# Three products of constants ahead of each turn of queries and of keys in the last batch of attention

## The chip, the cores and the metric

The kernel runs on one NeuronCore of one Trainium2 chip. The metric is the device time of one execution in microseconds (us); for each kernel the median of several runs is given. TensorE multiplies matrices, VectorE, ScalarE and GpSimd work on elements, and SyncE issues most of the DMAs. The five engines run their own instruction streams and wait for each other by semaphores. The results of TensorE land in PSUM, which has eight banks of 512 32-bit columns.

## The reference

The program computes a stack of six blocks on x of shape 4 x 512 x 256 (four batches of 512 tokens): half a mixture of experts (8 experts, the best 2 of each token), a causal attention with 16 heads of 16 columns and rotary positions, the same mixture of experts again, a gated feed-forward block with a Walsh-Hadamard transform, a linear attention on random features, and the feed-forward block again. Each block reads the layer-normalised x and adds to x. The change lies in the causal attention, which is, cut to what matters:

```
q, k, v = split((layernorm(x) @ Wqkv + bqkv).reshape(b, s, 3, H, hd))
q, k = rot(q), rot(k)
scores = einsum('bthd,bshd->bhts', q, k * scale) + causal_mask
ctx = einsum('bhts,bshd->bthd', softmax(scores), v).reshape(b, s, d)
x = x + ctx @ Wout + bout
```

Nothing that the change adds is read by any of this.

## The kernel before, in words

The stages run one after the other, each as a block of five instruction streams written out by hand. The attention stage is `attention_stage` (from L1129). It goes through the four batches, and in each batch through eight pairs of heads; a pair of heads is numbered w, 0 to 31 (`PAIR` is 8, `LAST` is 3, so the last batch is w = 24 to 31). A pair takes three steps t of one software pipeline (`STEPS` is 3): 24 steps a batch, 96 in all, and then a tail.

On TensorE the order is a fixed list (the loop `for t in range(ALL + LAG + 5)` in `_(pe)`). In each step it issues `scores(t)` (queries times keys, for the row maxima, L1440), `shifted(t - 7)` (the transposed scores, which ScalarE then takes the exponentials of, L1455), in two of six steps `weigh` (probabilities times values, L1470), then in the first step of a pair `turn_q(s + 1)` and in the second `turn_k(s + 1)`. A turn is four transposes of 128x128 blocks into PSUM bank 4 (L1411), which ScalarE (`out_q`, L1722) or VectorE (`out_k`, L1872) copies to where `scores` and `shifted` read it. The turns of pair w stand in the steps of pair w - 1, and `scores` of pair w waits for both copies. The turn of keys waits for ScalarE's copy of the queries, since both turns use bank 4. VectorE masks the scores in PSUM and takes their row maxima (`maxima`, L1882) into the stack of queries; `scores(t)` waits for the maxima of step t - 1 in the same bank, and `turn_q(w)` for all maxima of pair w - 2. Two more turns of queries, w = 32 and 33, follow the last pair: they carry only the maxima, as the shifts of the softmax.

Between these, TensorE does the work of other batches. In the first three batches the steps hold the projections of the next batch: `turn_x` (L1374), `project_qk` (28 products of 512 columns, L1386 and L1389) and `project_v` (24 of 256 columns, L1396). From the second batch on they hold the end of the batch before: `turn_sums` (L1480), `turn_context` (L1494), `project_half` (L1504). The last batch has no next batch to project. It has, instead, the first pieces of the experts stage that follows: `turn_after` of batches 0 and 1 (eight transposes each, L199) and `choice.logits_of` of the same (the router's logits, products of 8 columns, L235).

SyncE's queue holds, in order, for each w a wait for the copy of the queries of w + 2 and two small DMAs that place the shift (`place_shift`, L1257), and in the last batch between them the loads of the next stage's first weights (`early`, L1272).

`spin(nc, g, bank, count)` (L369) issues `count` products of a constant (`g.ident`) with a constant (`g.column`), 128x128 32-bit floats each, into the first 128 columns of a PSUM bank. Nothing reads the result. The kernel before calls it in several places where TensorE would stand idle. In the trace each such product is two MATMUL records of L372.

Of the kernel before, what the change touches and what calls it, by code (L numbers as in the profile page):

```python
# [48 lines left out]
def f32(ap):  # L49
    return ap.bitcast(F32)  # L50
# [318 lines left out]
def spin(nc, g, bank, count):  # L369

    for _ in range(count):
        nc.tensor.matmul(g.ps[:, bank, 0:P], g.ident[:, :], g.column[:, :], start=True, stop=True)  # L372
# [777 lines left out]
def attention_stage(nc, g, ins):  # L1150
# [3 lines left out]
    with ExitStack() as ctx:  # L1154
# [61 lines left out]
        PAIR = H // 2  # L1216
        CARRY = 2
        part = lambda j: sum((BT - a) * P for a in range(j))
        LAST = BATCH - 1
# [150 lines left out]
        def _(pe):  # L1370
# [36 lines left out]
            def turn_stack(w, stack, bank, done):  # L1407
                b, hp = w // PAIR, w % PAIR
                for i in range(BT):
                    flat = f32(stack[min(b, LAST) % 2][:, i, :, :]).rearrange("p h c -> p (h c)")  # L1410
                    last = nc.tensor.transpose(g.ps[:, bank, i * P:(i + 1) * P], flat[:, hp * P:(hp + 1) * P],  # L1411
                                               g.ident[:, :])
                last.then_inc(done, 1)

            def turn_q(w):
                pe.wait_ge(lo_done, 4 * min(w // PAIR + 1, BATCH))
                if w:
                    pe.wait_ge(k_out, min(w, BATCH * PAIR))
                if w >= CARRY:
                    pe.wait_ge(max_done, 2 * STEPS * (w - CARRY + 1))  # L1420
                if w > BATCH * PAIR:
                    pe.wait_ge(q_out, w)
                turn_stack(w, q_stack, 4, q_ps)

            def turn_k(w):
                pe.wait_ge(q_out, w + 1)
                turn_stack(w, k_stack, 4, k_ps)

            def scores(t):
# [110 lines left out]
            for i in (2, 3):  # L1540
                pe.wait_ge(lo_done, i)
                spin(nc, g, 0, 10)
            turn_q(0)
            turn_k(0)
            for t in range(ALL + LAG + 5):
                b, u = t // WIDTH, t % WIDTH
# [17 lines left out]
                if step == 0 and s + 1 < BATCH * PAIR + CARRY:  # L1564
                    turn_q(s + 1)
                elif step == 1 and s + 1 < BATCH * PAIR:
                    turn_k(s + 1)
# [1276 lines left out]
```

## Time and profile before

| what | value |
|---|---|
| median of 3 runs | 1104.36 us |
| lowest and highest run | 1098.37 and 1105.86 us |
| span of the profiled execution | 1103.5 us |
| mean granted clock of TensorE in it, of full speed | 0.935 |
| busy time of TensorE (share of the span) | 1021.3 us (93%) |
| of VectorE | 711.2 us (64%) |
| of ScalarE | 452.3 us (41%) |
| of GpSimd | 431.8 us (39%) |

The span runs from the first to the last instruction of one profiled execution; the page gives no other time of that execution. The busy time of TensorE counts each product from its start to its modelled end, so products that follow each other closely overlap, and the time that one more product takes is better read from the distance between starts. The granted clock is the share of full speed (2.4 GHz) at which TensorE was clocked; it is 1.00 or 0.50 at any moment, and a stretch with a value between them held both. Times in rows are from the start of the span.

### The profile page before, as it was taken

How to read it: one execution, taken by the hardware profiler on the slowest of the kernel's cores; microseconds unless marked ns; L12 is line 12 of the kernel's file. 1: busy time of each engine (PE TensorE's matmuls, PEld its weight loads, DVE VectorE, ACT ScalarE, POOL GpSimd, SP SyncE).
4: the chain of work that ended last, by engine and by line, in shares of the span. 5: the costliest groups of instructions: out<-in, count | busy, mean ns of one | idle time of the engine just before them, and what ended most of it. 6: DMA issues, size and time to landing. Idle time of an engine off the chain costs nothing. (4 is left out here: it accounts for less than half of the span.)

```text
span 1103.5 us, 18327 instructions
## 1 busy us (share of the span) xinstructions
PE 1021.3 (93%) x6383; PEld 845.2 (77%) x6383; DVE 711.2 (64%) x1740; ACT 452.3 (41%) x772; POOL 431.8 (39%) x473
## 2 busy tenths in 40 slices
PE   8889995799999999988999989999888998899997
PEld 7878885655566665577888878888778986888886
DVE  5854443988798876556554367765549977566654
ACT  4524332346675755535443312323344543223222
POOL 3246655326363621205566400000159987200000
PEclk7699997978999987888999999999988999999999
DMA  9224424200000023126542150000010300000000
GB/s 327 87 74 138 167 77 137 77 1 2 3 2 20 2 82 121 39 65 230 211 144 92 67 201 1 1 1 1 11 67 1 77 1 1 1 2 20 20 20 20
DMA packets 39179, 71.97 MB, mean 65 GB/s; under 512 B 10610, under 2 KB 28082, under 8 KB 38836
## 3 DMA queue, kind: packets, MB, share of 16 engines
q1 hardware_dynamic: 29492, 48.25, 13.3%
q0 software_dynamic: 7488, 20.46, 5.6%
q10 hardware_dynamic: 2112, 2.10, 0.6%
q8 instruction: 55, 0.90, 0.3%
q14 instruction: 32, 0.26, 0.1%
HBM read 46.78 MB, written 23.87 MB: 64 GB/s over the span
## 5 line engine op out<-in xcount | busy, mean ns | idle before, releaser
L2202 PE MATMUL ps<-xt,w 128*128 128x512 f32 x768 | 191.4, 399 | 4.1 <-PEq L437 2.7
L2202 PEld LDWEIGHTS ps<-xt,w 128*128 128x128 f32 x768 | 141.4, 190 | 34.4 <-DVE xt L210 4.5
L1882 DVE CUSTOM_DVE_ANT_0 ps<-ps,att_mask 128x128 f32<-128x128 f32 (+3 forms) x256 | 119.2, 517 | 28.2 <-PE ps L1440 27.8
L2296 DVE TENSOR_TENSOR had_gated<-ps,had_sig 128x512 f32<-128x512 f32 x64 | 44.3, 692 | 108.7 <-ACT had_sig L2255 108.7
L2255 ACT ACTIVATE had_sig<-ps 128x512 f32<-128x512 f32 x64 | 38.3, 599 | 185.2 <-PE ps L2202 185.2
L676 POOL DMA_INDIRECT moe_xs<-xn_rows,moe_index x78 | 85.3, 1093 | 71.1 <-DVE moe_index L1071 42.9
L1743 ACT ACTIVATE att_early_probs<-ps 128x384 f32<-128x384 f32 (+1 forms) x192 | 91.1, 528 | 51.8 <-PE ps L1455 51.2
L771 PE MATMUL ps<-moe_w,moe_narrow_xb 128*128 x390 | 110.8, 398 | 0.0
L155 POOL TENSOR_TENSOR var_eps<-bn,eps 128x4 f32<-128x4 f32 x22 | 4.7, 216 | 266.0 <-DVE bn L118 251.5
L682 POOL DMA_INDIRECT made_rows<-moe_units_made,moe_index x78 | 77.6, 995 | 71.2 <-ACT moe_units_made L919 59.6
L1331 POOL TENSOR_SCALAR_AFFINE_SELECT att_early_probs<-att_early_probs 128x256 f32<-128x256 f32 x128 | 54.6, 441 | 114.4 <-ACT att_early_probs L1743 114.1
L1090 DVE TENSOR_TENSOR moe_narrow_xb<-ps,moe_narrow_xb 128x512 fp32r<-128x512 f32 (+1 forms) x40 | 27.1, 678 | 110.8 <-ACT moe_narrow_xb L901 110.8
L2216 PE MATMUL ps<-w,had_yhi 128*128 128x256 f32 x512 | 94.4, 282 | 1.8 <-DVE had_ylo L2308 1.8
L2216 PEld LDWEIGHTS ps<-w,had_yhi 128*128 128x128 f32 x512 | 82.5, 188 | 7.9 <-DVE had_ylo L2308 2.6
L771 PEld LDWEIGHTS ps<-moe_w,moe_narrow_xb 128*128 128x128 f32 x390 | 73.8, 189 | 15.4
L901 ACT ACTIVATE moe_narrow_xb<-ps 128x512 fp32r<-128x512 f32 (+1 forms) x40 | 23.5, 587 | 131.6 <-PE ps L753 131.5
L1440 PE MATMUL ps<-att_kt,att_qt 48*128 48x128 f32 (+3 forms) x256 | 67.3, 439 | 9.6 <-DVE att_q_stack L1882 6.1
L2216 PE MATMUL ps<-w,had_ylo 128*128 128x256 f32 x256 | 71.7, 280 | 0.0
L372 PE MATMUL ps<-column,ident 128*128 128x128 f32 x364 | 55.4, 323 | 17.5 <-DMA back<-made_rows 11.4
L2440 POOL TENSOR_TENSOR fea_inv_norm<-fea_norm,neg_half 128x24 f32<-128x24 f32 x16 | 66.9, 4183 | 7.4 <-DVE fea_norm L2696 7.4
L372 PEld LDWEIGHTS ps<-column,ident 128*128 128x128 f32 x364 | 53.5, 236 | 18.5 <-DMA back<-made_rows 11.6
L1440 PEld LDWEIGHTS ps<-att_kt,att_qt 48*128 48x128 f32 x256 | 33.9, 204 | 41.6 <-issue 23.5
(290 smaller groups left out, 2326.1 us busy)
## 6 DMA issues: line engine op xcount, KB each, us to landing
moe_w<-in_moe SPq DMA_DIRECT2D x12, 768.0 KB, 8.0
back<-made_rows SPq DMA_DIRECT2D x14, 512.0 KB, 6.3
x<-x_turned SPq DMA_DIRECT2D x8, 512.0 KB, 6.9
low_weights<-moe_w SPq DMA_DIRECT2D x4, 768.0 KB, 3.6
w_early<-in_moe SPq DMA_DIRECT2D x4, 768.0 KB, 4.5
w_early<-low_weights SPq DMA_DIRECT2D x4, 768.0 KB, 11.4
x<-in_x SPq DMA_DIRECT2D x4, 512.0 KB, 5.6
xn_rows<-moe_wide_xn SPq DMA_DIRECT2D x4, 512.0 KB, 11.4
```

The source lines that it names most:

```text
L372: nc.tensor.matmul(g.ps[:, bank, 0:P], g.ident[:, :], g.column[:, :], start=True, stop=True)
L676: nc.gpsimd.indirect_dma_start(out=xs[:, j % AHEAD, i, :], out_offset=None, in_=g.xn_dram[:, :], in_offset=at(0, 2 * j + i)).then_inc(gath ...
L682: nc.gpsimd.indirect_dma_start(out=g.made_dram[:, :], out_offset=at(1, 2 * j + i), in_=made[:, j % 2, i, :], in_offset=None) \
L771: last = nc.tensor.matmul(h_bank(j, i), xb[a][:, j % 2, i, k, :], weight(c), start=False, stop=(k == KC - 1 and c == 1))
L1331: last = nc.gpsimd.affine_select(block, block, [[0, 2], [1, P]], ALU.is_ge, 0.0, base=0, channel_multiplier=-1)
L1440: last = nc.tensor.matmul(g.ps[:, a, col:col + n], qt[at, w % 4, i * P:n], kt[at, w % 4, 0:n], start=True, stop=True)
L1743: nc.scalar.activation(probs[:, w % 3, a, at:at + n], g.ps[:, 2 + a, 0:n], ACT.Exp, scale=HD ** -0.5).then_inc(exp_done, 1)
L1882: last = nc.vector.tensor_tensor_reduce(g.ps[:, a, col:col + n], g.ps[:, a, col:col + n], mask[:, SEQ - n:SEQ], -1.0, 3.0e38, ALU.add, ALU ...
L2202: last = nc.tensor.matmul(g.ps[:, bank(n, half), :], w[a][:, k, c * P:(c + 1) * P], xt[low][:, b % 2, k, :], start=(k == 0 and q == 0), st ...
L2216: last = nc.tensor.matmul(o, a[:, n % 4, at], g.w2[w][:, c, :], start=(c == 0 and q == 0 and i % 2 == 0), stop=(c == HC - 1 and q == 2), s ...
L2296: nc.vector.tensor_tensor(gated[:, n % 2, :], g.ps[:, bank(n, 0), :], sig[:, n % 2, :], ALU.mult) \
L2440: nc.gpsimd.tensor_tensor(inv_norm[:, t % 4, :], norm2[:, t % 4, :], g.neg_half[:, 0:QKH], ALU.pow) \
```

## The change

Ahead of the four transposes of a turn, and behind the waits of that turn, TensorE issues three products of constants into bank 4, for all turns with w over 24. These are the turns of queries for w = 25 to 33 and the turns of keys for w = 25 to 31. The turn of w = 24, which stands in the steps of the batch before, stays as it is.

```
@@ -1420,10 +1420,14 @@
                     pe.wait_ge(max_done, 2 * STEPS * (w - CARRY + 1))
                 if w > BATCH * PAIR:
                     pe.wait_ge(q_out, w)
+                if w > LAST * PAIR:
+                    spin(nc, g, 4, 3)
                 turn_stack(w, q_stack, 4, q_ps)
 
             def turn_k(w):
                 pe.wait_ge(q_out, w + 1)
+                if w > LAST * PAIR:
+                    spin(nc, g, 4, 3)
                 turn_stack(w, k_stack, 4, k_ps)
```

## Rows read from the trace of the kernel before

**Rows 1.** The page: span, and TensorE's granted clock in 40 slices, in tenths.
```profile
span 1103.5 us, 18327 instructions
PEclk7699997978999987888999999999988999999999
```

**Rows 2.** Busy time by stretch of the attention stage; the first row names the columns.
```profile
core 0: us, PE busy (x) PEld busy (x) DVE busy (x) ACT busy (x) POOL busy (x), PEclk, DMA share, GB/s
335.50:392.80 57.30, 56.16 (x431) 35.70 (x430) 48.88 (x170) 38.49 (x80) 30.07 (x51) 1.00 0.04 11
392.80:455.90 63.10, 60.15 (x415) 38.74 (x414) 44.91 (x185) 32.21 (x64) 13.88 (x34) 0.78 0.27 89
...
404.70:414.60 9.90, 9.17 (x36) 6.58 (x36) 7.87 (x37) 4.60 (x10) 2.00 (x5) 0.50 0.45 149
...
421.80:431.60 9.80, 9.19 (x48) 5.63 (x47) 8.41 (x39) 5.78 (x12) 2.15 (x6) 0.50 0.39 119
...
442.00:448.60 6.60, 6.60 (x39) 3.93 (x39) 3.74 (x10) 2.80 (x7) 1.17 (x3) 0.50 0.01 2
...
459.50:462.50 3.00, 3.00 (x24) 1.53 (x20) 2.04 (x6) 0.41 (x2) 1.27 (x2) 0.50 0.53 175
```

**Rows 3.** All waits of TensorE's products, 392.8 to 474: us, times, longest.
```profile
PE ps L1440 <- DVE att_q_stack L1882: 2.7, 7, 0.7
PE ps L1455 <- ACT att_early_probs L1743: 1.1, 3, 0.5
PE ps L1470 <- POOL att_early_probs L1331: 0.4, 1, 0.4
```

**Rows 4.** Timeline, TensorE at full clock: start us, us, engine, line, xcount.
```profile
361.74 1.44 PE L1389 MATMUL ps<-wqkv,att_xt 128*128 128x512 f32 x5
363.10 0.50 PE L1440 MATMUL ps<-att_kt,att_qt 48*128 48x128 f32 x4
...
386.60 0.66 PE L1411 MATMUL ps<-ident,att_q_stack 128*128 128x128 f32 x4
387.01 0.96 PE L1396 MATMUL ps<-wqkv,att_xt 128*128 128x256 f32 x6
387.90 0.45 PE L1440 MATMUL ps<-att_kt,att_qt 48*128 48x384 f32 x2
...
396.06 1.04 PE L199 MATMUL ps<-ident,att_turns_after_xn 128*128 128x128 f32 x8
397.03 0.50 PE L1440 MATMUL ps<-att_kt,att_qt 48*128 48x512 f32 x2
...
401.75 1.85 PE L235 MATMUL ps<-gate_w,att_qk 128*128 128x8 f32 x16
403.52 0.45 PE L1440 MATMUL ps<-att_kt,att_qt 48*128 48x384 f32 x2
```

**Rows 5.** Timeline, one turn of keys at half clock and the next instruction.
```profile
411.42 1.12 PE L1411 MATMUL ps<-ident,att_k_stack 128*128 128x128 f32 x4
412.33 1.91 PE L199 MATMUL ps<-ident,att_turns_after_xn 128*128 128x128 f32 x8
```

**Rows 6.** Timeline: ten products of constants at full clock.
```profile
209.58 2.50 PE L372 MATMUL ps<-column,ident 128*128 128x128 f32 x20
```

**Rows 7.** Busy time in a stretch that holds only products of constants.
```profile
504.80:507.90 3.10, 3.10 (x14) 3.10 (x15) 3.00 (x8) 2.32 (x3) 2.28 (x3) 0.50 1.02 424
```

**Rows 8.** Next stage's first weights: their loads and first reader (ns min/median/max, first, last start).
```profile
L845 ACT ACTIVATE moe_w<-w_early x4: 1467/1468/1474, 495.1 to 499.2; 128x1536 fp32r<-128x1536 f32 x4
...
L1272 SPq DMA_DIRECT2D w_early<-in_moe x4: 525/581/581, 403.8 to 428.9; - x4
```

More of the change, by code:

```diff
@@ L1422, in turn_q @@
                     pe.wait_ge(q_out, w)
+                if w > LAST * PAIR:
+                    spin(nc, g, 4, 3)
                 turn_stack(w, q_stack, 4, q_ps)
@@ L1426, in turn_k @@
                 pe.wait_ge(q_out, w + 1)
+                if w > LAST * PAIR:
+                    spin(nc, g, 4, 3)
                 turn_stack(w, k_stack, 4, k_ps)
```

## The prediction

> **What bounds the kernel now.** I read the page first, for the share of each engine and the granted clock by slices [rows 1]. The 15th to 17th slices (386 to 469 us), the last part of the attention stage, stand at 8, 7 and 8 tenths, where the four before them stand at 9. I then cut that part into stretches by the granted clock [rows 2]. The third batch, w = 16 to 23, took 57.3 us, at a clock of 1.00 throughout; TensorE was busy for 56.16 us of it and VectorE for 48.88. The last batch, w = 24 to 31, took 63.1 us, at a mean clock of 0.78. It holds three of the four stretches at half clock, 9.9, 9.8 and 6.6 us long; the fourth, 3.0 us, lies just behind it. TensorE was busy for 60.15 us of the 63.1. So in both batches TensorE bounds the stage by and large, and the last batch, which has less arithmetic on TensorE, is the longer one because of its clock. The list of waits says the same: from the start of the last batch to 474 us TensorE's products stood idle for 4.2 us behind named releasers, 2.7 of it for VectorE's maxima [rows 3].
>
> Inside the half-clock stretches the picture is mixed. In the first two VectorE was busy for 7.87 of 9.9 us and 8.41 of 9.8 us, so a faster TensorE would soon wait for it there; in the third it was busy for only 3.74 of 6.6 [rows 2].
>
> **What the change adds.** Nine turns of queries and seven of keys get three products each: 48 products. Ten of them at full clock are 20 records in 2.50 us [rows 6]; less about 0.27 for the end of the last record that is (2.50 - 0.27) / 19 = 0.117 us a record and 0.235 us a product. At half clock 14 records took 3.10 us [rows 7], 0.221 a record and 0.44 a product. A turn's three products cost 0.70 us at full clock and 1.33 at half; all 48 cost 11.3 us at full clock.
>
> They stand on TensorE's queue behind the waits of the turn and ahead of its transposes. Behind them wait the copy of the turned block (ScalarE for queries, VectorE for keys), and then `scores` of the next steps. Time spent here is therefore on the path unless TensorE would have waited just after. It did wait for 4.2 us in all [rows 3], and that is the most that the products can hide in as the trace stands. At full clock there would be more room in the first two slow stretches: 9.9 - 7.87 = 2.0 and 9.8 - 8.41 = 1.4 us are what VectorE leaves, and TensorE's 9.17 and 9.19 us would shrink to some 5 each, so that up to 4 us of products in each would lie beside VectorE's work.
>
> No DMA is issued by the change. SyncE's queue waits for copies of queries that come up to a fraction of a microsecond later per turn; the shifts it places are used several steps later, and no wait of TensorE names a DMA [rows 3]. The weights loaded from the same queue start at 403.8 to 428.9 us and are read first at 495.1 [rows 8]; a few us of delay cost nothing there, and tens would be needed to show.
>
> **What it gives back.** The clock. What stood ahead of the first fall, at 404.7, was the router's logits: 16 records of 8 columns, 1.77 us from start to the next start [rows 4], with TensorE called busy. Products of constants put full 128-column work beside them. In batch three the projections do the same service, and there the clock never fell [rows 2]. I take it that 11 us of products in place of 11 us of projections hold the clock as these did.
>
> **The sum, from batch three.** I build the new last batch out of batch three's 57.3 us at full clock. Distances of starts give the prices [rows 4]: five products of 512 columns take 363.10 - 361.74 = 1.36 us, 0.272 each, so 28 of them 7.6 us; six of 256 columns 0.89, so 24 of them 3.6; the eight transposes of the next batch 1.0 (eight others took 0.97). These 12.2 us fall away. The last batch has two sets of eight transposes (2 x 0.97) and two of logits (2 x 1.77), 5.5 us; it lacks one turn of keys, 0.4 (387.01 - 386.60). In it lie 15 of the 16 turns with products: 45 x 0.235 = 10.6. So 57.3 - 12.2 + 5.5 - 0.4 + 10.6 = 60.8 us, against 63.1 now: 2.3 us less. The sixteenth turn costs 0.7, and the fourth slow stretch behind the batch would shrink: a turn and its follower are 0.91 us apart at half clock [rows 5] and 0.41 at full [rows 4], other work less than twice, so I take 0.45 of the 3.0 us, 1.35. That is 0.65 less, together 3.0. Short bursts of projections come dearer by the product than a long one of constants, and short bursts of constants may too; with 0.1 us more for each of the 16 bursts, an estimate, it is 1.4 less. Between the two I take **2 us less**.
>
> **The same from the slow stretches.** TensorE's work in them is 9.17 + 9.19 + 6.60 + 3.00 = 27.96 us; at full clock it would shrink by at most 47%, 13.1 us. VectorE's work in them is 22.1 us of 29.3, so if VectorE bound them, 7.2 us would be gained. Gain 7.2 to 13.1, cost 11.3 less 0 to 4.2 hidden. The ends are -6.0 and +4.1 us; the sum from batch three lies between, and I take it, since it is of the same work at the same clock.
>
> I set it against the profiled execution, whose span is 1103.5; the median is 1104.36, 0.9 above, so the forecast is 1102.4 us, 2 us below the median.
>
> **A rule against it.** In the rows the clock fell at 404.7 although no wait of TensorE from 392.8 on was over 0.7 us [rows 3]. The Trainium skill, page "TensorE: Matmul & The Clock Gate", section "Why this matters for your kernels", ties the fall to idle gaps of over some 3 us between bursts. By that rule there is nothing here for the products to fill, and they could only cost. The trace does not agree with the rule as it stands. What it would make of the time is the third rival below.
>
> **The rivals.**
>
> *More is hidden.* With TensorE at full speed the first two slow stretches become VectorE's, and products lie in TensorE's waits. Then the low end above holds, -6: 1098.4 us. For it speaks VectorE's 7.87 of 9.9 us; against it, that in batch three, with VectorE at 85%, TensorE still had only 1.1 us free, and in the last batch VectorE has 44.91 us to do, 4 fewer. Chance 0.17.
>
> *One fall stays.* If the clock still falls once for some 9.9 us, behind the second logits for instance, 0.45 x 9.2 = 4.1 us of the gain are lost and about three turns cost 0.63 more each, 1.9: -2 + 6 = +4, 1108.4 us. Speaks for it that the falls hang on what happens to stand together. Chance 0.20.
>
> *The clock does not care* (the slower side). If products of constants do not keep it up, the same stretches stay slow. About 6 of the 16 turns lie in them. 6 x 1.33 + 10 x 0.70 = 15.0 us, less the at most 4.2 of waits, of which I take 3.0: +12, 1116.4 us. It decides where the stretch from 404.7 on stays at 0.50 with the products in it; two or more of the four stretches left slow bring it over 1108. Against it speak the full clock of batch three and of the stretch with ten products [rows 2, 6]. Chance 0.13.
>
> **How the numbers follow.** The forecast's own mechanism has 0.50, and gives 1102.4, with 1099 to 1107 around it. The rest of the kernel shifts by microseconds against whatever decides the clock elsewhere; 12 of 40 slices stand at 8 tenths or less [rows 1], and the runs of one kernel already lie 7.5 us apart. So I widen both ends: 1095 to 1113. A measurement of this kernel can tell about 1% (11 us) from no change. Faster by that means under 1093.3: only the first rival with luck elsewhere, 0.05. Slower means over 1115.4: the larger half of the last rival and a little of the third case, 0.09. Within 1%: 0.86.
>
> **What would show it.** Right: the granted clock is 1.00 from the start of the last batch to its end; the distance from the first `scores` of w = 24 to the end of its last is 61 to 63 us; the records of L372 grow by 96, each 0.117 us apart inside a turn; the waits of `scores` for VectorE's maxima are no longer than now. Wrong: slow stretches of together over 10 us remain there; or the clock is full and the batch takes under 58 us (products hidden) or over 65 (the copies behind the turns became the path, seen as VectorE and ScalarE waiting longer for L1411). Most likely to upset the forecast is the clock elsewhere: a stretch of the experts stage behind it that falls or is spared by its new place in time.

## The result: slower by half a per cent, where 2 us less were forecast

| | before | changed |
|---|---|---|
| median of 20 runs each | 1100.90 us | 1106.24 us |
| lowest and highest | 1093.61 and 1106.64 us | 1100.51 and 1113.45 us |
| ratio, 95% interval | | 1.0053 (1.0033 to 1.0073) |
| span of the profiled execution | 1103.5 us | 1106.6 us |
| mean granted clock in it | 0.935 | 0.948 |

The change costs 3.6 to 8.0 us. The device time of a run is 1.7 us over its span, so the profiled execution of before took 1105.2 us, 4.3 us above the median of the twenty: the forecast was built on one of the longer executions. That the changed kernel's 1106.24 us lies inside the stated 1095 to 1113 us is therefore in part luck: the kernel before runs 3.5 us faster than its first three runs said, and the change moved the time by +5.3 us where -2 was forecast. Of all runs in this document only four of the twelve of the version "ahead of scores" (1114.98 to 1115.85 us) were over 1.5% above its fastest and are left out of its row; with them its cost at equal clock would be 10.0 us in place of 8.9.

The profile after, page: the span, busy time and instructions by engine, and the clock granted by slice.

```profile
span 1106.6 us, 18519 instructions
...
PE 1021.0 (92%) x6479; PEld 849.5 (77%) x6479; DVE 711.8 (64%) x1740; ACT 452.6 (41%) x772; POOL 431.5 (39%) x473
...
PEclk7699997988999999988999999999998999999999
```

The 15th to 17th slices, 8, 7 and 8 tenths in [rows 1], are at 9 now. The clock did nearly what was forecast, and the kernel is slower.

The last batch is measured from here on from the first transpose of queries of w = 24 to that of w = 32: 386.60 us [rows 4] to 450.78 us before. The timeline of the changed kernel around these two marks, and one turn of queries with its products and the instruction behind it:

```profile
386.66 0.65 PE L1411 MATMUL ps<-ident,att_q_stack 128*128 128x128 f32 x4
...
393.43 0.94 PE L372 MATMUL ps<-column,ident 128*128 128x128 f32 x6
394.20 0.60 PE L1411 MATMUL ps<-ident,att_q_stack 128*128 128x128 f32 x4
394.73 0.73 PE L1444 MATMUL ps<-att_kt,att_qt 48*128 48x384 f32 x2
...
453.14 0.60 PE L1411 MATMUL ps<-ident,att_q_stack 128*128 128x128 f32 x4
```

A turn's three products take 0.77 us from start to the first transpose, not 0.70. The busy time of the engines between the marks, first before, then changed (columns as in [rows 2]):

```profile
386.60:450.78 64.18, 61.23 (x427) 39.85 (x423) 46.25 (x188) 32.60 (x65) 14.05 (x35) 0.79 0.26 88
```

```profile
386.66:453.14 66.48, 62.62 (x516) 44.77 (x513) 46.27 (x189) 32.80 (x65) 14.21 (x35) 0.97 0.26 85
```

Time at half clock in a stretch is its length times (1 - clock) times 2: 64.18 x 0.21 x 2 = 27.0 us before, 66.48 x 0.03 x 2 = 4.0 us after. So 23 us of half clock went away, and the batch still grew by 2.3 us. TensorE has 3.9 us without a busy record in it, against 1.1 in batch three [rows 2], and the waits of its products from 392.8 to 474 us, to be read beside [rows 3], are

```profile
PE ps L1444 <- DVE att_q_stack L1886: 3.2, 6, 0.9
PE ps L1459 <- ACT att_early_probs L1747: 1.3, 3, 0.7
PE ps L1474 <- POOL att_early_probs L1331: 0.4, 1, 0.4
```

They grew by 0.7 us. The products were put ahead of the turns, and the waits stand elsewhere, ahead of the scores.

The forecast named a sign for a batch of over 65 us at full clock: ScalarE and VectorE waiting longer for the turns. From the first scores of w = 24 to the turn of w = 33 the batch took 65.7 us, and the waits of ScalarE's and VectorE's copies for the transposes in that stretch, first before, then changed, are

```profile
ACT att_qt L1722 <- PE ps L1411: 6.6, 6, 1.5
DVE att_kt L1872 <- PE ps L1411: 2.1, 3, 0.8
```

```profile
ACT att_qt L1726 <- PE ps L1411: 12.2, 8, 2.2
DVE att_kt L1876 <- PE ps L1411: 2.8, 5, 0.9
```

So the copies behind the turns do start later. That alone does not say how much of the batch it cost.

### The profile page after: what moved, and what is told of

It is laid out like the page before. It is cut to its first block and busy times, and to the rows that moved or that the text cites. A ratio compares the mean times of both kernels' runs of the same rounds, so it can differ in the third digit from the quotient of the medians.

```text
span 1106.6 us, 18519 instructions
## 1 busy us (share of the span) xinstructions
PE 1021.0 (92%) x6479; PEld 849.5 (77%) x6479; DVE 711.8 (64%) x1740; ACT 452.6 (41%) x772; POOL 431.5 (39%) x473
## 3 DMA queue, kind: packets, MB, share of 16 engines
q1 hardware_dynamic: 29492, 48.25, 13.1%
## 5 line engine op out<-in xcount | busy, mean ns | idle before, releaser
L372 PE MATMUL ps<-column,ident 128*128 128x128 f32 x460 | 71.9, 321 | 17.3 <-DMA back<-made_rows 11.2
L372 PEld LDWEIGHTS ps<-column,ident 128*128 128x128 f32 x460 | 66.8, 231 | 24.5 <-DMA back<-made_rows 11.4
L1444 PE MATMUL ps<-att_kt,att_qt 48*128 48x128 f32 (+3 forms) x256 | 63.5, 416 | 10.9 <-DVE att_q_stack L1886 7.0
```

What stands on the lines that cost most here:

```text
L1444: last = nc.tensor.matmul(g.ps[:, a, col:col + n], qt[at, w % 4, i * P:n], kt[at, w % 4, 0:n], start=True, stop=True)
```

## The experiments

Two measures are used beside the ratio. One is the length of the last batch in the profile, with its time at half clock. The other comes from all runs: each run has a span and a mean granted clock, so a time at half clock over the whole program, span x (1 - clock) x 2. Over the runs of the kernel before in these experiments it goes from some 100 to 150 us, by itself, and the device time follows it with **0.283 us for each us at half clock** (112 of the 113 runs on record; 0.285 with all of them; standard error 0.013, correlation 0.9; mean 129.3 us at half clock, 1101.2 us of device time). The cost at equal clock in the table is the difference of the mean times less 0.283 times the difference of the mean half-clock times. The scatter of the runs about that line leaves each such cost uncertain by 0.8 to 1.5 us (95%). The slope comes from executions that differ by chance; that it also prices the half-clock time which products take away is an assumption. The first row is set against the mean of all runs of before in the experiments, since no clock is on record for the twenty runs of before in the section above.

| kernel | products | ratio (95%) | half clock, whole, us: this, before | cost at equal clock, us | last batch, us | half clock in it, us |
|---|---|---|---|---|---|---|
| changed | 48 | 1.0053 (1.0033 to 1.0073) | 113.2, 129.3 | +10.4 | 66.48 | 4.0 |
| changed, again | 48 | 1.0064 (1.0039 to 1.0089) | 115.9, 128.6 | +10.3 | 68.88 | 9.6 |
| before, again | 0 | 1.0018 (0.9994 to 1.0042) | 131.9, 128.6 | +0.6 | 64.18 | 27.0 |
| in batch three | 48 | 1.0104 (1.0063 to 1.0145) | 129.9, 129.9 | +11.0 | 63.39 | 24.1 |
| one a turn | 16 | 1.0021 (0.9995 to 1.0048) | 129.7, 129.9 | +2.5 | 63.55 | 16.5 |
| queries only | 27 | 1.0044 (1.0014 to 1.0074) | 125.3, 129.9 | +5.6 | 66.19 | 17.2 |
| keys only | 21 | 1.0062 (1.0035 to 1.0089) | 131.3, 129.9 | +6.3 | 64.96 | 6.5 |
| ahead of scores | 42 | 1.0025 (0.9990 to 1.0061) | 107.2, 128.6 | +8.9 | 64.05 | 0.0 |
| even scores | 12 | 0.9984 (0.9963 to 1.0005) | 117.0, 128.6 | +0.9 | 61.33 | 13.5 |
| even scores, again | 12 | 0.9962 (0.9939 to 0.9986) | 114.2, 131.0 | +0.5 | 61.35 | 13.5 |
| six a turn | 96 | 1.0123 (1.0080 to 1.0166) | 107.7, 128.1 | +21.0 | 75.40 | 3.0 |
| even scores and logits | 18 | 1.0000 (0.9974 to 1.0025) | 118.2, 128.1 | +2.9 | 61.81 | 7.4 |
| even scores, both | 21 | 1.0040 (1.0014 to 1.0066) | 138.4, 131.0 | +3.1 | 68.23 | 27.3 |
| short maxima | 0 | 0.9951 (0.9920 to 0.9982) | 128.5, 128.1 | -4.9 | 55.28 | 9.9 |
| short maxima, changed | 48 | 1.0008 (0.9978 to 1.0038) | 113.8, 128.1 | +5.7 | 62.04 | 3.7 |

**The price alone: the products in batch three.**

```
-                if w > LAST * PAIR:
+                if 2 * PAIR < w <= LAST * PAIR:
                     spin(nc, g, 4, 3)      # ahead of both turns
```

> The same 48 products (here 8 turns of queries and 8 of keys), but ahead of the turns of w = 17 to 24, in the batch whose clock is 1.00 anyway; none in the last batch. So it is the price without anything given back. Theory 1 (the products lie on the path almost whole, 0.77 us a turn as from start of the first product to start of the first transpose in the changed kernel): the third batch goes from 57.3 to 69.0 or more, the whole is 11 to 13 us slower than before. Theory 2 (VectorE's maxima leave room and products hide in it; the loss of the change is a wait elsewhere): the batch grows by 4 to 8 us and the whole by as much.

Measured: 1.0104, 11.0 us at equal clock. Batch three, from the first transpose of queries of w = 16 to that of w = 24, first before, then with the products in it:

```profile
329.32:386.60 57.28, 56.14 (x433) 35.69 (x429) 49.10 (x172) 38.48 (x80) 29.78 (x52) 1.00 0.04 11
```

```profile
327.37:393.35 65.98, 64.87 (x523) 45.40 (x520) 51.12 (x172) 38.98 (x80) 29.71 (x52) 1.00 0.03 10
```

It is 8.7 us longer than before, at a clock of 1.00 in both. Of the 48 products 45 lie between these marks (the last three, ahead of the turn of keys of w = 24, lie behind), so that is 0.19 us a product. That is less than the 11.7 of theory 1 for the batch and above theory 2; the whole is as theory 1 said, with an interval of 6.9 to 16 us. Nothing is given back here, so products at full clock cost most of their own length of 0.235 us.

**One product a turn.** `spin(nc, g, 4, 1)` in both places.

> One product ahead of each of the 16 turns in place of three. Theory 1 (each product costs its 0.235 us on the path, and the clock is held by a few of them): 32 products less, 7.5 us less than the changed kernel if the clock stays up, so 2 to 3 us faster than the kernel before; the last batch takes about 59 us. Theory 2 (the delay of the copies behind each turn costs, not the products' number): only 2 to 4 us less than the changed kernel. If one product doesn't hold the clock, slow stretches of 10 us or more come back and the time is that of the kernel before or above.

Measured: 1.0021, no gain. 16 products cost 2.5 us at equal clock, and the half-clock time of the whole is that of before (129.7 and 129.9 us). Theory 1's price is about right and its hope on the clock is wrong: one product a turn does not hold it. In the one profile the last batch had 16.5 us at half clock in place of 27.0, so it held in part there, but over all twelve runs nothing of it shows.

**Queries only, keys only.** The lines of the other turn taken out again.

> Three products ahead of the nine turns of queries, none ahead of keys. Theory 1 (every product on the path alike): 7 x 0.77 = 5.4 us less than the changed kernel, about as fast as the kernel before, if the clock is held. Theory 2 (products ahead of keys delay the copy of the keys that VectorE must make ahead of its maxima, and those ahead of queries hide beside the maxima): nearly all of the cost is saved, 8 us or more less than the changed kernel, 3 us faster than before.

> Three products ahead of the seven turns of keys, none ahead of queries. Theory 1: 9 x 0.77 = 6.9 us less than the changed kernel if the clock is held, 1 to 2 us faster than before. Theory 2: no more than 2 us less than the changed kernel, 3 us slower than before.

Measured: 1.0044 and 1.0062, against 1.0053 with both. At equal clock 27 products ahead of queries cost 5.6 us (0.21 each) and 21 ahead of keys 6.3 (0.30 each); with both, 48 cost 10.4. So all lie on the path, those ahead of keys perhaps a little more (each cost is uncertain by some 1.1 us), and theory 2's free place ahead of queries does not exist. What each half lost is the clock: the mean half-clock time is 125.3 and 131.3 us, with both 113.2. Half of the products cost half and gave back little, which is why leaving half out did not make the kernel faster.

**Both kernels again.** Unchanged.

> The kernel before, unchanged, for the spread of its clock and a second profile of its last batch. Theory A (the clock was overpriced): the last batch takes 57.9 us plus about 0.23 us for each us at half clock, as the profiles of before (64.2 us with 27.3 at half clock) and of the kernel with products in batch three (63.4 with 23.9) give; whatever half-clock time this profile shows, the batch lies on that line within 1 us. Theory B (the clock is worth 0.45 us a us): with 10 us less or more at half clock it takes 4.5 us less or more.

> The changed kernel, unchanged, for a second profile. Theory A: last batch 65 to 67.5 us with under 7 us at half clock, the whole 4 to 7 us slower than before. Theory B (the first profile of it was an unlucky one): the batch under 63 us.

The kernel before, from w = 24 to w = 32, in a second profile:

```profile
384.63:448.81 64.18, 61.22 (x427) 39.84 (x423) 46.28 (x188) 32.59 (x65) 14.05 (x35) 0.79 0.27 88
```

The same 64.18 us and the same 0.79 as in the first, so the falls of this batch recur; theory A's line is met, but so would theory B's be, since the half-clock time did not differ. The changed kernel was 1.0064 slower, as theory A had it, but its last batch took 68.88 us this time, above the range of theory A (and its 9.6 us at half clock are above the 7), with a fall behind the first logits that its first profile had not:

```profile
383.23:452.11 68.88, 65.65 (x516) 47.14 (x513) 46.29 (x189) 32.78 (x65) 14.16 (x35) 0.93 0.25 82
```

**42 products ahead of the scores.**

```
                     pe.wait_ge(k_out, w + 1)
                 for a in range(2):
+                    if step == 0 and w > LAST * PAIR:
+                        spin(nc, g, 4, 3)
```

> 42 products, in place of 48, moved to where TensorE waits for VectorE's maxima: three ahead of each of the two groups of scores in the first step of w = 25 to 31, none ahead of a turn. Theory A (products cost by their place: on the path ahead of a turn, hidden in the waits for the maxima): the last batch takes 58 to 62 us and the whole is 0 to 4 us faster than before. Theory B (42 products cost 0.17 to 0.26 us each wherever they stand): 7 to 11 us of cost, less 6 us of clock: 1 to 5 us slower than before.

Measured: 1.0025 (0.9990 to 1.0061), not told from none. In its profile the clock stayed full in the whole batch, and the batch was no shorter than before:

```profile
386.48:450.53 64.05, 63.10 (x510) 44.31 (x507) 46.31 (x189) 32.16 (x65) 14.17 (x35) 1.00 0.27 88
```

This one row refutes the forecast's base by itself: with everything at full clock and 42 x 0.235 = 9.9 us of products, the rest is at least 54.2 us. The forecast had 50.2 in its own stretch (60.8 less 10.6), which is 51.5 between these marks, since they take in six products of projections (0.9 us) and one turn of keys (0.4 us) more. Its waits for the maxima between the marks are

```profile
PE ps L1442 <- DVE att_q_stack L1884: 0.9, 4, 0.3
```

against 2.7 us before, so 1.8 us of products lay in them and the others on the path, which makes the rest 56.0 us; at equal clock over the whole the 42 cost 8.9 us, 0.21 each. For odd w `weigh` stands ahead of the scores and there is no wait to hide in. Theory A was half right.

**12 products ahead of the scores of w = 26, 28 and 30.**

```
                     pe.wait_ge(k_out, w + 1)
+                    if w > LAST * PAIR and w % 2 == 0:
+                        spin(nc, g, 4, 4)
```

> 12 products in all: four ahead of the first scores of w = 26, 28 and 30, where the changed kernel's trace has TensorE waiting 0.94, 0.93 and 0.53 us for the maxima. Theory A: they cost nothing there; if they spare one or two of the falls the batch takes 60 to 63 us and the whole is 1 to 4 us faster than before; if they spare none it is the same as before. Theory B: 2 to 3 us slower than before unless a fall is spared.

> The kernel with 12 products ahead of the first scores of w = 26, 28 and 30 once more, to narrow its interval (0.9963 to 1.0005 so far) and for a second profile of its last batch. If the forecast's base (50.2 us at full clock without products) were right, a batch with 12 hidden products and x us at half clock would take 50 + 0.45 x; with the base that the step from three to six products gives (57 to 58 us, some 0.28 a us at half clock) it takes 57 + 0.28 x, 61 us with 14 us at half clock. Whole: 1 to 3 us faster than before, or no difference.

Measured: 0.9984 and, with fresh runs, 0.9962 (0.9939 to 0.9986). In the second the interval excludes no change: 1.5 to 6.7 us faster than the kernel before, and the first agrees. At equal clock it costs 0.9 and 0.5 us, not told from nothing, and the half-clock time of the whole is 12 and 17 us shorter. The last batch in the second profile:

```profile
382.55:443.90 61.35, 59.52 (x451) 40.01 (x447) 46.41 (x189) 32.38 (x65) 14.15 (x35) 0.89 0.28 92
```

Here the place matters: these are the scores that the changed kernel still waits ahead of,

```profile
408.54 0.88 PE L1444 MATMUL ps<-att_kt,att_qt 48*128 48x128 f32 x3 [0.94 <-DVE att_q_stack L1886]
...
425.65 0.88 PE L1444 MATMUL ps<-att_kt,att_qt 48*128 48x128 f32 x3 [0.93 <-DVE att_q_stack L1886]
...
440.80 0.88 PE L1444 MATMUL ps<-att_kt,att_qt 48*128 48x128 f32 x3 [0.53 <-DVE att_q_stack L1886]
```

It is the one version that computes the whole attention and beats both kernels. It did not spare every fall: in the second profile the first of its three bursts already runs at half clock, behind the first logits (2.00 us from the first of its eight records to the scores behind them):

```profile
402.21 2.07 PE L372 MATMUL ps<-column,ident 128*128 128x128 f32 x8
404.21 0.80 PE L1442 MATMUL ps<-att_kt,att_qt 48*128 48x128 f32 x4
```

**Six products a turn.** `spin(nc, g, 4, 6)` in both places.

> Six products ahead of each of the 16 turns in place of three: 48 more, at a clock that the three already held nearly. The growth of the last batch from three to six is the price of a product without anything given back, and the batch of the changed kernel less that growth is the last batch at full clock without any. Theory 1 (each product on the path, 0.235 us): 45 more in the batch make it 77 us, so 56 us without any; the whole is 10 to 12 us slower than the changed kernel. Theory 2 (a third hidden): 74 us, and 59 without any. The forecast had 50.2 us for that batch.

```profile
386.54:461.94 75.40, 72.05 (x606) 54.76 (x603) 46.29 (x189) 32.80 (x65) 14.16 (x35) 0.98 0.22 75
```

Measured: 1.0123; 48 more products cost 10.6 us more at equal clock (21.0 less 10.4), 0.22 each. Between the marks 45 more at practically the same clock lengthen the batch by 75.40 - 66.48 = 8.9 us, 0.198 each. Taking the first 45 off the changed kernel at that price leaves **57.6 us, with 4.0 at half clock, for the last batch without products**. It lies between the two theories (56 and 59). That the first 45 cost what the next 45 cost is not shown; at 0.22 each it would be 56.6. Against the 64.18 us of before, with 27.0 at half clock, the clock is then worth (64.18 - 57.6) / 23.0 = 0.29 us a us, close to the 0.283 that the runs give for the whole program (0.33 with 56.6).

**Even scores, and three more ahead of the turns of queries of w = 26 and 28.**

> The 12 products ahead of the first scores of w = 26, 28 and 30, and three more ahead of the turns of queries of w = 26 and 28, which stand just before the two sets of router logits: 18 in all. Theory 1 (what holds the clock is full products near the stretches that lack them; six on the path cost 1.4 us): the fall behind the first logits is spared, 2 to 3 us, so the batch takes 59 to 61 us and the whole is 2 to 5 us faster than before. Theory 2 (the number counts): falls of 10 us or more remain, and the whole is within 1 us of before.

Measured: 1.0000, where theory 1 had 2 to 5 us of gain. The batch took 61.81 us with 7.4 at half clock: 6 us of half clock fewer than with the 12, and nothing gained, since the six products on the path cost as much (2.9 us at equal clock in place of 0.5 to 0.9).

**Four and three products, ahead of both groups of scores of w = 26, 28 and 30.**

> Four products ahead of the first and three ahead of the second group of scores in the first step of w = 26, 28 and 30: 21 in all, seven together, where the trace shows TensorE waiting for the maxima of both groups. If the base is 57 to 58 us and these hide, the batch takes 58 to 61 us with 0 to 10 us at half clock, and the whole is 2 to 4 us faster than before. If the second group no longer has a wait to hide in, three times 0.7 us come on top and nothing is won against the 12 products.

Measured: 1.0040 (1.0014 to 1.0066), slower. The half-clock time is 27.3 us in the batch, as without any products, and 138.4 over the whole, where the kernel before had 131.0 beside it. Its first bursts run at half clock too, as the first of the 12 products did:

```profile
407.54 2.07 PE L372 MATMUL ps<-column,ident 128*128 128x128 f32 x8
409.54 0.79 PE L1442 MATMUL ps<-att_kt,att_qt 48*128 48x128 f32 x2
410.27 1.65 PE L372 MATMUL ps<-column,ident 128*128 128x128 f32 x6
411.84 0.47 PE L1442 MATMUL ps<-att_kt,att_qt 48*128 48x128 f32 x1
```

More products did not mean more clock. Neither theory had this, and no run here says what kept the clock down.

**Short maxima, without and with the products.** VectorE's maxima in the last batch over the last 128 columns of each row alone; this kernel leaves the rest of the row out of the maximum:

```
+                        m = P if t >= LAST * WIDTH else n
                         last = nc.vector.tensor_tensor_reduce(
-                            g.ps[:, a, col:col + n], g.ps[:, a, col:col + n], mask[:, SEQ - n:SEQ],
+                            g.ps[:, a, col + n - m:col + n], g.ps[:, a, col + n - m:col + n], mask[:, SEQ - m:SEQ],
```

> The kernel before, with VectorE's maxima in the last batch over the last 128 columns alone (the rest of the row is left out of the maximum), so that VectorE is no longer near its limit there. If VectorE's chain sets the length of the last batch beside TensorE, as I now think, the batch shortens by 4 us or more at the same clock. If TensorE's own work sets it (the forecast's view), it shortens by no more than the 2.7 us of waits for the maxima.

> The changed kernel with the same short maxima in the last batch (128 columns of each row; the rest left out of the maximum). With VectorE out of the way the products have nothing to hide beside: 45 of them cost 10.6 to 11.6 us in the batch, and against the kernel with short maxima and no products it is longer by that less 0.25 to 0.45 us for each us of half clock spared. If VectorE's waits had hidden nothing in the changed kernel either, the difference between the two pairs (with and without products) is the same, about 2 to 4 us.

Between the marks, without and with the products:

```profile
385.99:441.27 55.28, 54.29 (x426) 36.31 (x423) 34.91 (x188) 32.27 (x65) 13.99 (x35) 0.91 0.30 102
```

```profile
386.49:448.53 62.04, 60.11 (x517) 43.62 (x513) 35.01 (x189) 32.59 (x65) 14.28 (x35) 0.97 0.27 91
```

VectorE's busy time falls from 46.25 to 34.91 us, and the batch from 64.18 to 55.28. Of these 8.9 us the clock is 17.1 x 0.29 = 5.0; the other 3.9 are VectorE's. Over the whole it is 4.9 us at equal clock (uncertain by 1.2), with a mean half-clock time like that of before, so this figure does not hang on what the clock is worth. That is more than the 2.7 us of waits, so VectorE's chain is part of what sets the batch, as the first alternative said. The products cost 5.7 + 4.9 = 10.6 us at equal clock here, and 10.4 in the changed kernel: shortening the maxima did not change their price, so VectorE's maxima had not hidden them before either.

## Why the prediction was wrong

**What bounds the kernel: half right.** TensorE has the most to do in both batches, and the falls of the clock recur. But in the last batch VectorE's maxima, in the loop scores, maxima, next scores, set 4 to 5 us of the length; the list of waits names 2.7 of them.

**The cost: right.** The forecast had 48 x 0.235 = 11.3 us, nearly all of it on the path. Measured at equal clock: 10.4 and 10.3, and 11.0 in batch three, where no clock was given back.

**The clock: right in kind.** It is 1.00 from 392.8 to 442 us in the first profile, with 4.0 us at half clock between the marks where 27.0 were. The second profile has 9.6 us. The second rival, one fall that stays, has its condition nearly met in that execution, with a fall of some 7 us from 407 us on: it had +4 us for the whole, and the batch was 4.7 us longer than before. Its reason does not hold, since the first profile, without that fall, was not 2 us faster either. The fourth slow stretch, behind the batch, did go, but another came: there 32 records of `weigh` at 470.12 us took 3.74 us where they took 2.35 before. From the transposes of w = 33 to the next stage's (L199) it is 14.51 us, 14.85 before, so of the 1.35 us that the forecast gained behind the batch 0.3 came.

**"The sum, from batch three" is the step that failed.** It took 12.2 us of projections out of a batch of 57.3 us as if the batch shortened by all of it, and arrived at 50.2 us for the last batch at full clock without products, 51.5 between the marks. Measured by taking products off at their own price it is 57.6 with 4.0 us at half clock, 56.4 at none; the version with 42 products at full clock gives 56.0. So some 5 us of the expected gain were never there.

The starts of the changed kernel's records say where the sum and the batch part, in the forecast's own stretch, 392.82 to 458.51 us. Each time is from the start of a group to the start of the next, less the waits that the timeline names:

| term | forecast, us | changed kernel, us |
|---|---|---|
| batch three | 57.3 | 57.3 |
| projections and their transposes, gone | -12.2 | -13.0 |
| transposes and logits of the next stage | +5.5 | +5.5 |
| turns, against batch three's | -0.4 | +0.9 |
| waits ahead of scores, 3.2 against batch three's 0.8 | 0 | +2.4 |
| products of constants, 15 bursts | +10.6 | +12.2 |
| scores, shifted scores, `weigh` | 0 | +0.4 |
| sum | 60.8 | 65.7 |

The term that the forecast put at nothing is the largest: it took over batch three's waits, 0.8 us, and TensorE waits four times as long ahead of its scores here, for VectorE's maxima. The bursts are next (0.77 us for 0.70, and two of the fifteen wholly or in part at half clock), then the turns (0.53 us where scores follow at once, and one at half clock). That VectorE's chain sets part of the batch is shown: with its maxima shortened, the batch without products is 3.9 us less at the same clock. That in batch three the projections stood beside that chain, so that taking them away leaves time that TensorE cannot use, fits this and the waits (3.9 us without a busy record of TensorE in the changed kernel's last batch, 1.1 in batch three), but no run took projections out of batch three or shortened its maxima.

**"The same from the slow stretches" had the answer at one end.** It bounded the gain by 7.2 us, if VectorE bound those stretches, and 13.1 if TensorE did. The profiles give 64.18 - 57.6 = 6.6 us in the batch, at the low end. The sum chose -2 between -6 and +4.1 us; the batch came out at +2.3 and +4.7 us, the sixteenth turn at 0.7 more. The value of half-clock time, 0.45 us a us, came from rows of TensorE's own work. Over whole runs it is 0.283. The Trainium skill, page "TensorE: Matmul & The Clock Gate", section "Terms", prices it at the throttled time times (1 - K/N), where K/N is the granted clock, so 0.5 for each us at half clock here. The runs of this kernel give 0.283. That the other engines catch up while TensorE is slow would explain it; it is not shown by itself.

**The whole.** The mean half-clock time fell from 129.3 to 113.2 us, worth 16.1 x 0.283 = 4.6 us, and the mean time grew by 5.9 us, so the products cost 10.4. That is how this cost was worked out and no test of it. The tests are the 11.0 us of batch three, at the same mean half-clock time, and the 10.6 us of 48 more products.

**The first rival** (more is hidden) falls with the price: 10.4 us at equal clock is 0.22 a product, nearly its whole length. **The rule against the change** (falls come from idle gaps alone, so products could only cost) forecast full cost without a gain, +12. The change lost for another reason: the gain was there, and was smaller than its price.

## What to carry to other kernels

To price a faster clock, do not scale TensorE's busy time in the slow stretches; regress the time of the runs on their granted clock, or take the bound that the next engine leaves. A batch that does the same work with less beside it is not shorter by what is missing, if what is missing filled another engine's time: remove it in thought only down to that engine's chain. And in this kernel products of constants paid only where TensorE waits: 12 of them in its waits gained 2 to 4 us, 48 on its path lost 5 to 7.

## What was not expected of the hardware

The half-clock time of one kernel differs between executions by some 50 us over the program (clock 0.931 to 0.953), and explains most of the spread of its runs, 1092.9 to 1109.0 us. The place of products mattered more than their number: 12 ahead of even scores went with 114 to 117 us at half clock over the whole, 21 around the same scores with 138, 16 spread over the turns with 130. In three profiles of other versions (the kernel before, 12 and 21 products around even scores) the first fall stands right behind the first router logits; in the changed kernel's first profile and with 42 products ahead of scores none stands there. What decides a fall stays open; that would need the clock's own record against many placements, and was not tried.
